# Order of the activation's transposes and the down projection in a mixture-of-experts pipeline

## The reference

```
x = x + layernorm(linear_attention(layernorm(x)))      # 16 heads, elu+1 features, Wo
x = x + layernorm(moe(layernorm(x)))

moe: logits = x @ wg.T; top 8 of 32 experts by softmax, weights renormalised
     for each expert e, for its rows:
        h = silu(x @ w1[e]) * (x @ v1[e])               # 512 -> 192, twice
        y = (h @ w2[e]) * weight_of_the_row             # 192 -> 512
     out[token] += y
```

## Time and profile before

| | |
|---|---|
| median of 3 runs | 2549.44 us (2547.16 to 2557.21) |
| the profiled execution's own time | 2549.61 us |
| its span | 2547.9 us |
| PE busy, whole span | 2263.1 us (89%) |
| DVE, ACT, POOL busy | 1574.4, 1305.3, 952.4 us |
| stage of the experts' tiles | 1216 to 2477 us of the span |
| PE busy in that stage | 1147.2 us of 1261 us |
| mean granted clock in that stage | 0.96 |

### The profile page before, as it was taken

One profiled execution on the slowest core, in us unless ns is written; L12 is line 12 of the kernel. 1 busy time (PEld: TensorE's weight loads), 2 busy tenths in 40 slices (PEclk: granted clock), 3 DMA queues, 4 the chain that ended last, 5 costly groups with the idle time before them and its releaser, 6 DMA issues.

```text
span 2547.9 us, 69695 instructions
## 1 busy us (share of the span) xinstructions
PE 2263.1 (89%) x11804; PEld 1931.4 (76%) x11805; DVE 1574.4 (62%) x4968; ACT 1305.3 (51%) x2786; POOL 952.4 (37%) x1130
## 2 busy tenths in 40 slices
PE   7999899999989999982898889878999898989990
PEld 5887588888868888871797788767898787977980
DVE  4455567777767777763465656555565555656546
ACT  3343556666656656641455555444555554555443
POOL 1112025555535555555133333323333332333342
PEclk9999999999999999995899999989999998999995
DMA  3334113232333333336688877777786777877778
GB/s 117 94 114 114 58 34 127 106 125 106 129 125 120 120 112 126 108 114 212 158 138 178 173 156 166 166 197 161 149 155 133 179 152 181 140 175 143 135 137 289
DMA packets 164993, 358.13 MB, mean 141 GB/s; under 512 B 21184, under 2 KB 21184, under 8 KB 164800
## 3 DMA queue, kind: packets, MB, share of 16 engines
q0 software_dynamic: 60224, 144.21, 28.5%
q1 hardware_dynamic: 104704, 213.21, 28.1%
HBM read 178.21 MB, written 179.14 MB: 140 GB/s over the span
## 4 chain that ended last, share of the span: by engine, by line
PE 26%; DMA 12%; issue 6%; SPq 5%; DVEq 2%; ACT 1%; DVE 1%; POOL 1%; ACTq 1%; POOLq 0%
DMA BIG<-sorted_rows 9%; PE bank L465 5%; PE bank L466 5%; PE bank L467 5%; PE bank L454 3%; DMA moe_sum<-X,aidx 3%; SPq L329 2%; PE bank L482 1%; PE bank L483 1%; PE bank L484 1%; PE bank L486 1%; PE bank L485 1%; PE bank L475 1%; ACT BIG L598 1%; SPq L348 1%
## 5 line engine op out<-in xcount | busy, mean ns | idle before, releaser
L1479 POOL DMA_INDIRECT moe_sum<-X,aidx x274 | 428.5, 1564 | 868.3 <-issue 504.4
L959 PE MATMUL bank<-WB,XH 128*128 128x512 f32 x1536 | 478.5, 393 | 0.0
L465 PE MATMUL bank<-WB,XL 128*128 x1096 | 405.2, 370 | 8.8 <-issue 2.9
L466 PE MATMUL bank<-WB,XH 128*128 x1096 | 379.0, 346 | 0.0
L467 PE MATMUL bank<-WB,XH 128*128 x1096 | 378.8, 346 | 0.0
L959 PEld LDWEIGHTS bank<-WB,XH 128*128 128x128 f32 x1536 | 290.5, 189 | 60.0 <-issue 0.5
L959 PE MATMUL bank<-WB,XL 128*128 128x512 f32 x768 | 316.2, 412 | 10.7 <-DVE XL L1266 10.7
L959 PE MATMUL bank<-WB,SH 128*128 128x512 f32 x1024 | 319.0, 393 | 0.0
L1545 POOL DMA_INDIRECT sorted_rows<-srow,pos x256 | 266.4, 1041 | 95.4 <-issue 95.4
L736 DVE SCALAR_TENSOR_TENSOR BIG<-BIG,bank x274 | 95.1, 347 | 322.6 <-ACT BIG L535 234.5
L546 ACT ACTIVATE X<-bank (+1 forms) x276 | 165.1, 598 | 240.7 <-POOLq L845 122.4
(11 more groups left out here) (219 smaller groups left out, 4454.9 us busy)
## 6 DMA issues: line engine op xcount, KB each, us to landing
BIG<-sorted_rows SPq DMA_DIRECT2D x278, 274.0 KB
X<-x_in SPq DMA_DIRECT2D x64, 256.0 KB, 2.8
RAW<-w_in SPq DMA_DIRECT2D x16, 768.0 KB
LATE<-w_in SPq DMA_DIRECT2D x16, 768.0 KB
sorted_rows<-BIG SPq DMA_DIRECT2D x33, 274.0 KB, 5.1
moe_sum<-LATE SPq DMA_DIRECT2D x34, 256.0 KB, 3.0
LATE<-x_in SPq DMA_DIRECT2D x32, 256.0 KB, 3.1
RAW<-wo_in SPq DMA_DIRECT2D x16, 512.0 KB, 3.4
```

Source lines behind the costliest of these rows:

```text
L465: nc.tensor.matmul(eu[s][:, 0:UP], XL[:, s, k, :], wh, start=k == 0, stop=False)
L466: nc.tensor.matmul(eu[s][:, 0:UP], XH[:, s, k, :], wh, start=False, stop=False)
L959: last = nc.tensor.matmul(ps, w, m, start=start and i == 0, stop=stop and i == len(terms) - 1)
L1479: nc.gpsimd.indirect_dma_start(acc_dram[:, :], bass.IndirectOffsetOnAxis(aidx[:, s:s + 1], 0), rows, None, compute_op=ALU.add).then_inc(s_ ...
```

## The change

In each turn PE does `down(g-2)` ahead of `act_t(g-1)`; ACT does `evacuate(g-2)` ahead of `act_high(g-1)`; DVE does `add_index(g-2)` ahead of `act_low(g-1)`. After the loop PE's last pair is turned round in the same way. No instruction is added or removed, and all waits keep their counts.

```diff
@@ moe_pe @@
                     rows_t(g + 1, 1 - s)
                     up(g, s, e, now)
+                    down(g - 2, s, before)
                     act_t(g - 1, 1 - s)
-                    down(g - 2, s, before)
 
             total = 2 * pairs
             rows_t(total + 1, 1)
+            down(total - 2, 0, experts_at(total)[2])
             act_t(total - 1, 1)
-            down(total - 2, 0, experts_at(total)[2])
             down(total - 1, 1, experts_at(total + 1)[2])
@@ moe_act @@
                     silu(g, same)
+                    evacuate(g - 2, same)
                     act_high(g - 1, other)
-                    evacuate(g - 2, same)
                     rows_high(g + 2, same)
@@ moe_dve @@
                     gate(g, same, e)
+                    add_index(g - 2, same)
                     act_low(g - 1, other)
-                    add_index(g - 2, same)
                     rows_low(g + 2, same)
```

## The result

The changed kernel takes 2573.45 us (median of 4 runs, 2569.06 to 2584.27) beside 2548.3 us for the kernel before (4 runs): the ratio is 1.0098, with a 95% interval of 1.0058 to 1.0138. It is slower, by 25 us between the medians; 2586 had been forecast. The profiled execution took 2569.06 us and its span is 2567.4 us, 19.5 us more than before; what the traces show has to add up to these 19.5.

What follows compares the result with a forecast made beforehand. The prediction took PE to bound the experts' tiles, its sequencer barely ahead. Sequencer 26, late adds 12, late gates 5 and given back -7 sum to 36 us on 2549.6: 2586 us, range 2546 to 2620.

Steps and rivals of the forecast that it cites:

- What bounds it: Experts' tiles: PE sets the pace, 3.89 us a tile, its sequencer about 0.15 us ahead in the branch tile; attention untouched.
- PE's work: PE in each tile: same 23 matmuls and transposes, switching between kinds of transpose has no price, 0 us.
- ACT and DVE: Steady tiles: `evacuate` then `act_high` on ACT make DVE's `act_low` end 1.35 us into the next turn, 0.37 us later.
- PE's sequencer: Steady tile pairs: longer hold for `act_low` delays the next `up` by 0.35 us, 74 pairs, 26 us.
- Late adds: `evacuate` waiting for POOL now also delays `act_high`, `act_low` and PE's `down`: 12 us, bounds 0 and 54.
- Late gates: PE's 12 waits for the late gate L739: `act_low` later and `act_t` behind it, 5 us, bounds 0 and 10.
- The waits for L739: Sign in the profile after: number and length of PE's waits for the gate L739 should stay.
- Given back: Expert changes ending with ACT waiting for weights from DRAM: PE's earlier loss is not lost twice, -7 us.
- The lead suffices: Rival, PE's sequencer: its lead covers the later `act_low`, no change, 2550 us; chance 0.17.
- `down` fills the wait: Rival, late gates: PE does `down` while the gate is late, faster, 2534 us; chance 0.08.
- The adds hold PE: Rival, waits for POOL: most of 54 us land on PE, slower, 2620 to 2640 us; chance 0.10.
- The clock: Rival, PE's clock: falls more often through six transposes in a row or many small gaps, 2646 us; chance 0.02.

Runs made afterwards that it cites:

- one read behind or ahead: Changed kernel plus one extra table-word read by PE's sequencer in one turn of two, behind or ahead of its wait for `act_low`: 2633.82 us behind, 2595.29 us ahead.
- TensorE's part alone: Kernel before with only PE's `down` moved ahead of `act_t`, ACT and DVE in the old order: 2568.25 us, ratio 1.0072.
- ScalarE's part alone: Kernel before with only ACT's `evacuate` moved ahead of `act_high`, PE and DVE in the old order: 2607.96 us, ratio 1.0226.
- the change with fewer waits: Changed kernel without three PE waits that an earlier PE wait already covers (in rows_t, up and act_t): 2560.79 us, ratio 1.0041.
- the kernel before with fewer waits: Kernel before without the same three covered PE waits in rows_t, up and act_t: 2553.18 us, ratio 1.0005.

## Why the prediction was right

**What bounds it.** Right: the attention kept its time, PE is the pace of the steady tiles, and its sequencer was the nearest thing to a second bound.

**PE's work, 0 us.** Right: the chain gives 0.22 and 0.44 us for the transposes, as before, now side by side.

**ACT and DVE.** Right to a few hundredths: `evacuate` 3.63 us into the tile (3.65 at the median), `act_high` 0.49 behind it, `act_low` starting 0.93 (measured 0.94) and ending 1.35 (1.36) into the next turn. This is the turn that ends with the branch; in the other, whose own start is late, it ends at 1.03 (median). The idle time before L746 was to be a wait for L540; the profile names L540 for 69 of these waits and "issue" for 204.

**PE's sequencer, 26 us.** Right: 27.5 us in the intervals under 4.4 us, tiles alternating 3.91 and 4.23 where 3.9 and 4.25 were forecast, 140 waits of L465 on issue with 47.1 us where about 140 and 50 were. The runs with three operations less, and with one read behind or ahead, show that it is the work behind the wait. What the step lacked is that the sequencer as a whole has only some 0.45 us left in two tiles.

**Late adds, 12 us.** Too high. The mechanism is there; a tile of the changed kernel shows it whole:

```profile
2302.86 0.60 ACT L546 ACTIVATE X<-bank  x1 [2.86 <-POOLq L845]
2303.36 0.38 ACT L540 ACTIVATE SH<-bank  x1
2304.18 0.42 DVE L746 TENSOR_TENSOR SL<-bank,SH  x1 [1.03 <-ACT SH L540]
...
2304.96 0.49 PE L482 MATMUL bank<-WB,SL 128*128 x1 [1.62 <-DVE SL L746]
```

POOL lets `evacuate` go late, and `act_high`, `act_low` and PE's `down` come late one behind the other; PE loses 1.6 us. But only four of the 28 waits of `down` for `act_low` are of this kind, 3.3 us together, and the waits of `evacuate` for POOL fell from 120.1 us in 64 to this:

```profile
ACT X L546 <- POOLq L845: 73.3, 32, 4.0
```

The prediction had X and index ready sooner, so that adds start sooner. The kernels with one part each don't bear that out. TensorE's part alone first, then ScalarE's:

```profile
ACT X L546 <- POOLq L845: 63.6, 38, 3.2
...
ACT X L546 <- POOLq L845: 144.0, 73, 4.8
```

In the same window, 1216 to 2520 us, they are 122.4 us in 65 waits before and 75.5 in 33 after. The fall comes with TensorE's part, where `evacuate` starts later in its turn than before (4.22 us instead of 3.86, medians of steady tiles), so it does not need an earlier X. That later start shortens 65 waits by at most 23 us, not 59: the reason of the rest stays open.

**Late gates, 5 us.** Too small by the trace: 24 of the 28 waits of `down` for `act_low` are late gates, 36.8 of the 40.1 us; before, PE waited 20.5 us for the gate and then 5.7 us at L482, so these waits grew by 10.6 us, a little over the upper bound of 10. The waits for L739 did not stay, as the prediction's sign had it: they moved to L482. Doing `down` first filled none of it, as argued.

**Given back, -7 us.** Not shown. ACT's waits for weights, where it was put, fell from 25.8 to 20.5 us. PE's waits for rows fell more: 77.7 us before, 61.1 after. With 24 us taken off the steady tiles again (the change with fewer waits) they rose to 70.3 us, and in the kernel before with fewer waits they are 89.8. One could read from this that where DMA sets when rows arrive at a change of expert, a PE that comes later waits less. But with ScalarE's part alone, the slower kernel, they are 78.5 us, as much as before. No run removed the rows' lateness, and each trace is one execution: the reading stays open.

**The sum.** 26 + 12 + 5 - 7 = 36 us had been forecast, 25 by the medians (19.5 by the profiled executions) came. The steady term is 27.5. All else together was forecast at +10; it is -8 in the traces and about -2 by the medians, with an interval of 10 us to each side. So the steady term carries the forecast. Of the small terms, late adds were 9 us too many and late gates some 6 too few; that these two partly cancel is luck.

**The rivals.** "The lead suffices" did not come true, nor what the prediction drew from the Trainium skill, page "Advanced Engine Details and Errata", section Engine Queue Depths (a queue of 64 instructions on TensorE): the sequencer stands at L482 while it is held, and of 0.37 us of lateness with the issue of `act_t` behind it, 0.33 us a pair reach PE. "`down` fills the wait" fell with the 40.1 us above. *The adds hold PE* fell with the four tiles. The clock stayed at 0.96 in the stage with six transposes in a row.

One row of the changed profile misleads: 288.5 us of the gate's (L736) idle time are put down to `act_t`. The gate starts 3.88 us into the tile (3.87 before, medians of steady tiles), so the change of name did not move it. The semaphore named is the one that came last in time.

## What to carry to other kernels

In a loop whose addresses are computed at run time, find for each engine which wait holds its sequencer and how much the sequencer has to do behind it before the next matmul: a value that arrives "long before it is needed" by the engine's timeline can be just in time for the sequencer. A step that looks free because all engines have idle time is priced by that lead, here 0.15 us. And a remainder of a few microseconds should not be read from one trace of each kernel: here executions of one kernel differ by 10 us and more, and what the steady tiles don't explain stays open.

## What was unexpected of the hardware

PE's sequencer needs about 7.35 us of operations for two tiles with 46 matmuls and transposes, 94% of the time that PE needs for them. One wait or address operation takes about 0.1 us; one read of a table word with its decoding added 0.64 us, 0.3 of it the read itself. Several waits for the same semaphore and value in a row became a single one, and a wait that could ride on another operation became one of its own when a second wait took that place, which alone cost 0.26 us in a pair of tiles.
